# An audio tower's attention stage: rounds written out, and the latent product of a step moved behind the queries of the same step

## The reference, cut to what matters

```
q_c = rmsnorm(hidden_states @ w_qa, g_qa)               # rank 384
q = (q_c @ w_qb).reshape(b, s, 32, 192).transpose(0, 2, 1, 3)
q_nope, q_rope = (q[..., :128], q[..., 128:])
kv = hidden_states @ w_kva
k_c, k_rope = (kv[..., :128], kv[..., 128:])
k_c = rmsnorm(k_c, g_kva)
kst = (k_c @ w_kvb).reshape(b, s, 32, 256).transpose(0, 2, 1, 3)
k_nope, v = (kst[..., :128], kst[..., 128:])
q_rope = q_rope * cos + rotate_half(q_rope) * sin
k_rope = k_rope * cos + rotate_half(k_rope) * sin
scores = einsum(concat(q_nope, q_rope), concat(k_nope, k_rope)) * 192 ** -0.5
attn = softmax(scores, axis=-1)
out = einsum(attn, v)
return out.reshape(b, s, 32 * 128) @ w_o
```

## Time and profile before

| | us |
|---|---|
| runs | 2131.76, 2132.52, 2133.24 (median 2132.52) |
| the profiled execution | 2130.34 |
| its span, first to last instruction | 2128.6 |
| busy in the span: PE, DVE, ACT, POOL | 1938.4 (91%), 1314.6 (62%), 757.9 (36%), 279.4 (13%) |
| attention stage, first to last latent product | 510.49 to 1882.47 |

### The profile page before, as it was taken

One profiled execution on the slowest core, in us unless ns is written; L12 is line 12 of the kernel. 1 busy time (PEld: TensorE's weight loads), 2 busy tenths in 40 slices (PEclk: granted clock), 3 DMA queues, 4 the chain that ended last, 5 costly groups with the idle time before them and its releaser, 6 DMA issues. The chain is left out here.

```text
span 2128.6 us, 42839 instructions
## 1 busy us (share of the span) xinstructions
PE 1938.4 (91%) x11794; PEld 1066.4 (50%) x11794; DVE 1314.6 (62%) x2805; ACT 757.9 (36%) x2051; POOL 279.4 (13%) x612
## 2 busy tenths in 40 slices
PE   4788888768999999999999999999999999959999
PEld 1344445444555555555555555555555555525554
DVE  3666666635666666666666666666666666656664
ACT  3344444323333333333333333333333333332221
POOL 2354444320000000000000000000000000023332
PEclk8899999979999999999999999999999999979999
DMA  5112211003332222222232222322222121243332
GB/s 137 40 40 47 49 42 38 19 3 95 55 68 55 55 55 69 54 52 54 55 73 55 55 52 54 69 55 55 55 67 55 37 43 38 40 137 75 83 80 69
DMA packets 250560, 123.82 MB, mean 58 GB/s; under 512 B 240272, under 2 KB 240528, under 8 KB 248336
## 3 DMA queue, kind: packets, MB, share of 16 engines
q1 hardware_dynamic: 246192, 94.71, 20.7%
q10 hardware_dynamic: 4320, 28.51, 4.3%
HBM read 56.07 MB, written 8.39 MB: 30 GB/s over the span
## 5 line engine op out<-in xcount | busy, mean ns | idle before, releaser
L1090 PE MATMUL out_ps<-m_h,ot_h 128*128 (+1 forms) x1024 | 389.0, 380 | 4.1 <-DVE ot_l L889 4.1
L1092 PE MATMUL out_ps<-m_h,ot_l 128*128 (+1 forms) x1024 | 388.8, 380 | 0.0
L1091 PE MATMUL out_ps<-m_l,ot_h 128*128 (+1 forms) x1024 | 388.7, 380 | 0.0
L939 DVE SCALAR_TENSOR_TENSOR resid<-out_ps,resid 128x512 f32 (+1 forms) x256 | 177.1, 692 | 309.7 <-PE out_ps L1092 308.6
L804 ACT ACTIVATE ot_h<-av_ps 128x512 f16<-128x512 f32 x128 | 76.4, 597 | 762.5 <-PE av_ps L1112 762.5
L1281 POOL MEMSET fpower<- 128x1 f32 x1 | 0.1, 99 | 1426.3 <-POOLq L717 1426.3
L868 ACT ACTIVATE prob<-s_ps,nmx 128x128 f32<-128x128 f32 x512 | 180.1, 371 | 5.7 <-DVE nmx L965 5.7
L1090 PEld LDWEIGHTS out_ps<-m_h,ot_h 128*128 128x128 f16 x1024 | 100.4, 98 | 129.9 <-issue 13.9
L1091 PEld LDWEIGHTS out_ps<-m_l,ot_h 128*128 128x128 f16 x1024 | 100.4, 98 | 129.5 <-issue 19.1
L1092 PEld LDWEIGHTS out_ps<-m_h,ot_l 128*128 128x128 f16 x1024 | 100.3, 98 | 121.2 <-issue 0.8
L960 DVE TENSOR_REDUCE mx<-s_ps 128x4 f32<-128x512 f32 x128 | 88.5, 692 | 63.9 <-PE s_ps L1075 63.9
(11 more groups left out here) (239 smaller groups left out, 4014.5 us busy)
## 6 DMA issues: line engine op xcount, KB each, us to landing
wide<-heads_in ACTq DMA_DIRECT2D x30, 928.0 KB, 5.4
wide<-x_in SPq DMA_DIRECT2D x32, 512.0 KB, 6.0
tower_out<-result SPq DMA_DIRECT2D x16, 512.0 KB, 2.6
stage<-wb_in SPq DMA_DIRECT2D x8, 512.0 KB, 8.3
resid<-wqk_in SPq DMA_DIRECT2D x1, 2304.0 KB, 11.8
zt<-z SPq DMA_TRANSPOSE x128, 2.4
turned<-halves SPq DMA_TRANSPOSE x128, 3.0
wide<-heads_in SPq DMA_DIRECT2D x2, 928.0 KB, 4.6
```

Of the source, the lines that this page charges most:

```text
L939: dve.scalar_tensor_tensor(out=resid[:, at], in0=out_ps[hf][:, :], scalar=1.0 / (O_S * M_S), in1=resid[:, at], op0=ALU.mult, op1=ALU.add). ...
L1090: pe.matmul(out_ps[hf][:, :], ot_h[:, h, :], m_h[:, at], start=h == 0, stop=False)
L1091: pe.matmul(out_ps[hf][:, :], ot_h[:, h, :], m_l[:, at], start=False, stop=False)
L1092: last = pe.matmul(out_ps[hf][:, :], ot_l[:, h, :], m_h[:, at], start=False, stop=h == HEADS - 1)
```

## The change

Every engine but SP gets its 32 rounds written out one behind the other, without a loop. In a step the latent product moves: it stands behind the queries and products of its step and takes that step's own probabilities, and the outputs of the step before stand ahead of the queries. ScalarE and VectorE take the halves of the latent result (ot_h, ot_l) at the end of the step, not in the next one; VectorE adds the two output halves to the residual ahead of the low half of the queries, not at the end. SP turns z and the probabilities of the same step in turn, in one loop over the steps. The arithmetic is the same.

```diff
--- before.py
+++ after.py
@@ -766,37 +766,31 @@
                 body(at(-1), at(0), at(1), more)
 
             start()
-            run(0, True)
-            with eng.Fori(1, ROUNDS - HEADS - 2, 2) as t:
-                run(t, True, 1)
-                run(t + 1, True, 0)
-            run(ROUNDS - HEADS - 1, True)
-            with eng.Fori(ROUNDS - HEADS, ROUNDS - 1) as t:
-                run(t, False)
-            run(ROUNDS - 1, False)
+            for t in range(ROUNDS):
+                run(t, t < ROUNDS - HEADS)
 
         @block.sync
         def _(sp):
             def turn_rope(s):
-                wait_apart(sp, sp_passed, (z_lo, s + 1))
+                waits = [(z_lo, s + 1)]
                 if not isinstance(s, int) or s >= 1:
-                    wait_apart(sp, sp_passed, (s_done, s))
+                    waits.append((s_done, s))
+                wait_apart(sp, sp_passed, *waits)
                 sp.dma_start_transpose(zt[:, :, :], z[:, :, :].rearrange("p h n -> p (h n)")
                                        ).then_inc(zt_turned, 16)
 
             def turn_prob(s):
-                wait_apart(sp, sp_passed, (p_lo, s + 1))
+                waits = [(p_lo, s + 1)]
                 if not isinstance(s, int) or s >= 1:
-                    wait_apart(sp, sp_passed, (av_done, s))
+                    waits.append((av_done, s))
+                wait_apart(sp, sp_passed, *waits)
                 sp.dma_start_transpose(turned[:, :, :], halves[:, :]).then_inc(p_turned, 16)
 
             turn_rope(0)
-            turn_rope(1)
             turn_prob(0)
-            with sp.Fori(1, ROUNDS * QUAD - 1) as s:
-                turn_rope(s + 1)
+            with sp.Fori(1, ROUNDS * QUAD) as s:
+                turn_rope(s)
                 turn_prob(s)
-            turn_prob(ROUNDS * QUAD - 1)
 
         @block.scalar
         def _(act):
...
@@ -859,8 +847,6 @@
                     load(now.t + HEADS + 1, 1 - now.parity)
                 for j in range(QUAD):
                     s = now.slot + j
-                    if before or j:
-                        latent_high(now.slot + (j - 1), not before and j == 1)
                     act.wait_ge(max_step, s * 2 + 2)
                     if before or j:
                         act.wait_ge(p_lo, s)
@@ -878,8 +864,10 @@
                         query_high(after, j)
                     if more and j:
                         prod_high(now.t + HEADS, now.parity, now.side * -1 + 1, now.place, j - 1, prod_ps, False)
-                if not after:
-                    latent_high(now.slot + (QUAD - 1), False)
+                    act.wait_ge(av_done, s + 1)
+                    if before or j:
+                        act.wait_ge(out_done, s * 2)
+                    high(ot_h[:, :, :].rearrange("p h n -> p (h n)"), av_ps[:, :], O_S / (PR_S * KC_S), o_hi)
 
             rounds(act, start, body)
 
...
@@ -963,8 +945,6 @@
                     if before or j:
                         dve.wait_ge(exp_done, s * 4)
                     dve.tensor_scalar(nmx[:, :], mx[:, :], -EXP_SCALE, None, ALU.mult).then_inc(max_step, 1)
-                    if behind[0]:
-                        latent_low(now.slot + (j - 1))
                     if after or j < QUAD - 1:
                         rotate(s + 1)
                     dve.wait_ge(exp_done, s * 4 + 4)
@@ -973,21 +953,24 @@
                     dve.tensor_tensor(prob[:, :, :], prob[:, :, :],
                                       rrec[:, :, None].broadcast_to([P, HEADS, P]), ALU.mult
                                       ).then_inc(norm_step, 1)
+                    behind = (now, j - 1) if j else (before, QUAD - 1)
                     if after or j < QUAD - 1:
                         rope_low(s + 1)
                     dve.wait_ge(p_hi, s + 1)
                     if before or j:
                         dve.wait_ge(p_turned, s * 16)
                     low(p_l, prob[:, :, :].rearrange("p h n -> p (h n)"), PR_S, p_h, p_lo)
+                    if behind[0]:
+                        add_out(*behind, 0)
+                        add_out(*behind, 1)
                     if after:
                         query_low(after, j)
                     if more and j:
                         prod_low(now.t + HEADS, now.parity, now.side * -1 + 1, now.place, j - 1, prod_ps)
-                    if behind[0]:
-                        add_out(*behind, 0)
-                        add_out(*behind, 1)
+                    dve.wait_ge(o_hi, s + 1)
+                    low(ot_l[:, :, :].rearrange("p h n -> p (h n)"), av_ps[:, :], O_S / (PR_S * KC_S),
+                        ot_h[:, :, :].rearrange("p h n -> p (h n)"), o_lo)
                 if not after:
-                    latent_low(now.slot + (QUAD - 1))
                     for hf in range(2):
                         add_out(now, QUAD - 1, hf)
                     dve.wait_ge(out_added, ROUNDS * 8)
@@ -1100,38 +1083,37 @@
                     queries(Round(pe, 0), h, (qp_ps, av_ps)[h % 2], 1)
                 rope(Round(pe, 0), 0)
 
...
             def body(before, now, after, more):
                 operands = score_operands(now, 0)
                 for j in range(QUAD):
-                    behind = (now, j - 1) if j else (before, QUAD - 1)
+                    s = now.slot + j
                     scores(now, j, operands)
-                    if behind[0]:
-                        latents(*behind)
-                    if j < QUAD - 1:
-                        rope(now, j + 1)
-                    elif after:
-                        rope(after, 0)
+                    if after or j < QUAD - 1:
+                        if j < QUAD - 1:
+                            rope(now, j + 1)
+                        else:
+                            rope(after, 0)
+                    if before or j:
+                        if j:
+                            outputs(now, j - 1)
+                        else:
+                            outputs(before, QUAD - 1)
                     if after:
                         queries(after, j)
+                    if j < QUAD - 1:
+                        operands = score_operands(now, j + 1)
                     if more and j:
                         products(now.t + HEADS, now.parity, j - 1, prod_ps, (now.t + HEADS) * 3 + (j - 1))
-                    if behind[0]:
-                        outputs(*behind)
-                    if j < QUAD - 1:
-                        operands = score_operands(now, j + 1)
+                    if before or j:
+                        pe.wait_ge(o_lo, s)
+                    at = bass.ds(now.tok + j * P, P)
+                    probs_h, probs_l = (turned[:, at, :].rearrange("p h n -> p (h n)")
+                                        for at in (slice(0, HEADS), slice(HEADS, 2 * HEADS)))
+                    pe.wait_ge(p_turned, s * 16 + 16)
+                    pe.matmul(av_ps[:, :], kc_h[:, at], probs_h, start=True, stop=False)
+                    pe.matmul(av_ps[:, :], kc_l[:, at], probs_h, start=False, stop=False)
+                    pe.matmul(av_ps[:, :], kc_h[:, at], probs_l, start=False, stop=True).then_inc(av_done, 1)
                 if not after:
-                    latents(now, QUAD - 1)
                     outputs(now, QUAD - 1)
 
             rounds(pe, start, body)
```

## The result

The changed kernel takes 2097.81 us (median of 4 runs, 2097.37 to 2099.74) against 2132.14 for the one before beside it (2131.09 to 2133.24): 34.3 us less, a ratio of 0.9841 with a 95% interval of 0.9824 to 0.9858. The direction was forecast, and the range holds it; the forecast of 2111 stands 13 us too high, just outside its own case (2098 to 2124), and rival 1's 2101 is the number nearest to it.

The account below looks back on a forecast made before the run. TensorE was taken to bound the attention stage. Intervals of 1338.4 against 1371.98 us save 33.6, less 2 for the clock and 10.4 for new code: net 21, so 2111 us against the median; range 2092 to 2150.

Parts of the forecast that it names:

- rival 1: New code is hidden on every engine, so only 2 us come off the gain: 2101 us; chance 0.22.
- its own case: The forecast's likeliest case, 2111 us with a span of 2098 to 2124; chance 0.43.
- The bare steps: TensorE's undisturbed attention steps: 9.87 us for j=0, 10.54 for j=1, 10.73 for j=2 and j=3, 41.87 a round.
- Part 1, the "issue" gaps: Writing rounds out removes TensorE's j=0 issue gaps, 0.77 us and some shorter ones in each of 26 loop rounds.
- Part 2, the chain of 10.26 us: From one latent product to the next through softmax and transpose: 10.26 us, bounding j=0 and covered at j=1 to 3.
- The waits that move: Reordered waits: ot_l in time, last queries 0.4 us each in rounds 29 to 31, zt fits with 0.4 us.
- The head load's collision: ScalarE's head load moves behind ot_h, so its collision with zt and turned goes: up to 0.78 us a round.
- The clock in step 0: TensorE idles in step 0 and its clock may drop to 1.2 GHz: 2 us lost, between 0 and 4.
- the charge for new code: On SP, one 0.95 us too long transpose issue in each of 32 rounds, half on turned: 10.4 us, 0 to 30.
- The low end of the range: 2092 us, for a chain of 10.2 us and nothing lost at step 0 or to new code.
- Rival 2: Every round's long issue falls on turned with no spare, costing 30 us: 2131, give or take 8; chance 0.14.
- Rival 3: On SP zt behind turned becomes the last wait, the chain is 11.2 us, 52 us more, 2184; chance 0.17.

Follow-up runs that it names:

- the fifth experiment: Rounds written out in the old step order, with ScalarE holding the next head's load until the previous step's turned halves have landed; 2079.85 us, 0.9758 of the kernel before.
- the third experiment: The changed kernel with a second, equal maximum of the scores ahead of the one that counts; 2139.4 us in a single run.
- the fourth experiment: The changed kernel with SP's order of before, zt of the next step issued ahead of turned; 2113.35 us in a single run.
- Part 1: The kernel before with its rounds written out, the order of its step and SP's loop kept; 2109.09 us, 0.9885 of the kernel before.
- the last experiment: The changed kernel with the next head's load issued behind the high half of the probabilities of j=0; 2134.34 us, 1.0005 of the kernel before.

## Why the prediction was right, and where it was not

Seven kernels make a table, in us:

| | load beside the transposes | load clear of them |
|---|---|---|
| loop, order of before | 2132.1 (before) | 2094.6 |
| written out, order of before | 2109.1 | 2079.9 |
| loop, new order | | 2127.5 |
| written out, new order | 2134.3 | 2097.8 (the change) |

The empty cell was not tried. By the differences, writing the rounds out is worth 15 to 30 us, getting the load off the transposes 29 to 38, and the new order by itself **costs** 18 written out with the load clear (2097.8 against 2079.9), 25 with it beside and 33 in the loop. The change is faster because it writes out the rounds (2132.1 to 2109.1) and because its order puts the load clear of turned, which is worth more than the order costs (2109.1 to 2097.8).

**The bare steps** held: 10.54, 10.73 and 10.73 came out as 10.53, 10.73 and 10.73, and 9.87 for j=0 stands in the fifth experiment.

**Part 1, the "issue" gaps**, held: none is left. In the old order writing out was worth 14.8 us with the load clear, 23 with it beside; the prediction has no sum for it apart.

**Part 2, the chain of 10.26 us**, held as the mechanism, and the third experiment shows it: it bounds j=0 and covers the rest. It measures 10.11, 0.15 less. Half of that is the reason the working named, an instruction that starts a little before the last one's time is over: the maximum starts 0.08 us before the end of ot_l. The other half, 0.07, is on SP, where the change also joins two waits ahead of turned into one; the working took 0.86 from the old code. ScalarE's and VectorE's timelines at the boundary, answering to the earlier trace rows:

```profile
1011.29 0.60 ACT L798 ACTIVATE ot_h<-av_ps 128x512 f16<-128x512 f32 x1
...
1011.92 0.69 DVE L877 SCALAR_TENSOR_TENSOR ot_l<-av_ps,ot_h 128x512 f16<-128x512 f32 x1
1012.53 0.68 DVE L942 TENSOR_REDUCE mx<-s_ps 128x4 f32<-128x512 f32 x1
...
1013.45 0.37 ACT L854 ACTIVATE prob<-s_ps,nmx 128x128 f32<-128x128 f32 x1 [1.56 <-DVE nmx L947]
...
1016.59 0.69 DVE L877 SCALAR_TENSOR_TENSOR halves<-prob,halves 128x512 f16<-128x512 f32 x1 [0.36 <-ACT halves L798]
```

From the start of the latent product at 1010.45: ot_h after 0.84, ot_l 0.63 on, the maximum already 0.61 behind it and not 0.69, the first exponential 0.92 on, the low half of the probabilities 3.14, the issue of turned (1017.38) 0.79 and not 0.86, the product 3.18. At 27 steps of j=0 and 16 without products 0.15 each makes 6.5 us.

**The waits that move**: the output product waits for ot_l at no step of a round, as said. zt fits behind turned, and the fourth experiment shows that turned is the wait that ends last. Rounds 29 to 31 take 10.70 at j=0 where 10.66 was said, but over a chain that is shorter: the wait for the last queries is worth 0.59 and not 0.4. The head load's collision goes, as said, and with more room: the load is issued 0.90 us behind the latent product and not 1.9, and lands 4.7 later, ahead of turned's issue at 6.93. But its worth was understated: "up to 0.78 us a round" is the difference of two intervals of one round, and holding the load back took 39.5 us out of the loop kernel, 1.5 for each of the 26 loads that stood at a boundary. Within the sum this did no harm, since the sum went from the bare steps up and not from the collision down.

**The clock in step 0** was put at 2 us and measures 2.5.

**The step that failed is the charge for new code**, "one in each of 32 rounds", 10.4 us. In the changed kernel's attention stage no transpose behind the first zt takes over 1.24 us to issue, though every round's code is new. The queue rows of its page show how much more code is fetched:

```profile
q8 instruction: 79, 1.29, 0.3%
q14 instruction: 51, 0.42, 0.1%
```

From 505 to 1880 us of the twelve traces there are 2662 transposes with neither a head load nor a code packet in flight, and they land within 3.24 us (turned) and 2.45 (zt); 223 land later than 3.3 and 2.7, and each of these has a load or a code packet beside it.

What failed is the rate. From the fourth experiment's kernel, SP's and TensorE's timelines and the code packet between 903 and 904 us:

```profile
902.43 1.19 SPq L778 DMA_TRANSPOSE zt<-z  x1
903.80 2.19 SPq L785 DMA_TRANSPOSE turned<-halves  x1
...
q8 instruction: 1, 0.02, 9.0%
...
896.42 0.38 PE L1113 MATMUL av_ps<-turned,kc_h 128*128 128x512 f16 x1 [0.47 <-DMA turned<-halves]
907.97 0.38 PE L1113 MATMUL av_ps<-turned,kc_h 128*128 128x512 f16 x1 [0.85 <-DMA turned<-halves]
```

Both transposes land 4.0 us behind their issue, and the step takes 11.55 us in place of 10.57. In the changed kernel 68 packets of q8 come in the stage, and not one meets turned: each starts within 5.6 us behind a latent product and is over by 6.54, and turned is issued at 6.93. In the written-out kernels of the old order 14 to 18 meet it. Part 1's four intervals of 12.7 to 13.0 us have one beside the load, and the fifth experiment's three longer rounds have one; elsewhere in those rounds turned had time to spare.

Why the packets keep to the first half of a step in the new order is not shown, and that they cause the late landings is argued from their meeting, not tested. The Trainium skill's page "Runtime: NRT & Kernel Launch", section "Instruction fetch mechanics", calls such a crossing mostly hidden. The changed kernel agrees with it; the 11.55 us above are a step in which a fetch was not hidden, by way of a transpose. Rival 1, built on that rule, gave 2101: its number is near, and its reason is borne out as far as no fetch meets turned here.

So the sum of the intervals was to be 1338.4 + 2 + 10.4 = 1350.8 and is 1334.74. The 16.1 us between are the 10.4 that were not there and the 6.5 of the chain, less 0.5 of clock, about 16.4. Outside the intervals the sum put nothing, and 4.2 us came on there, so the forecast against the profile, 2109, was too high by 12 and not by 16. The low end of the range does not follow from its own words: a chain of 10.2 and nothing lost make 2096, not 2092; the result lies inside either way.

**Rival 2** fell with the charge. **Rival 3**, slower by zt behind turned, did not come: zt, 1.67 us behind turned on SP, was never late after step 0. Yet the rival's picture, a transpose that is late beside other traffic, is what the last experiment shows, with turned as the one that TensorE waits for and the head load as the traffic.

## What to carry to other kernels

Before reordering a step around a late transfer, look at what else is on the DMA engines when it is issued: holding one bulk load by a single wait, until the latency-bound transfers of the step have landed, gave here as much as the whole change, and more together with the written-out rounds. Where a change alters two things, price each by the kernel that has one alone, and build a stage's time from its undisturbed steps up; the difference then names what is still lost. A rare long event needs two things before it is a price: what stood beside it each time, and how often the two will meet in the new order. Here the first was right and the second was a guess.

## What was unexpected of the hardware

In the last experiment a 928 KB load beside two transposes cost them far more than itself: turned went from 3.18 to 4.65 us from issue to use, while the load's median to landing was 4.8 us there and 4.7 in the changed kernel. They come from two queues, ScalarE's and SP's; the Trainium skill's page "DMA: Bandwidth & Descriptors", section "Issuing engines are not separate DMA queues", says that such transfers run on the same 16 engines and interleave, and the late landings agree with it. SP's own issue is longer as well: in the last experiment zt's took 1.32 to 1.84 us in 26 of the 27 rounds with a load (1.62 in the row shown), against 1.19 in nearly all the others.

The loop's "issue" wait is not one number: with the load out of the way it alternates between 0.53 and 0.22 us in the two rounds of the loop's body, and is nearly gone in round 27, which is written out behind the loop (9.98 us for its j=0). Rounds 28 to 30, a loop again but without products and loads, show none of it (9.87 at j=0), so a loop alone does not bring it.
